# One factor chain for two layer norms in a fused attention and expert kernel, with ScalarE's normalizations at other steps

## The reference

```python
x = layernorm(x + attention(x))      # 16 heads of 8, causal
# feed-forward:
xn = (x - mu) / sqrt(var + 1e-5) * gamma + beta
combine, idx = top2_gate(xn, Wg)     # 8 experts, two for each token
out = sum_e gate_e * (gelu(xn @ W1[e] + b1[e]) @ W2[e] + b2[e])
x = layernorm(x + (x + out))
```

## Time and profile before

| what | value |
| --- | --- |
| median of 3 runs | 1116.17 us (1111.87 to 1117.45) |
| the profiled execution | 1118.13 us |
| its span, first to last instruction | 1116.4 us |
| PE busy | 966.8 us (87%) |
| DVE busy | 830.4 us (74%) |
| ACT busy | 665.9 us (60%) |
| POOL busy | 683.8 us (61%) |
| mean granted TensorE clock | 0.964 of full speed |

### The profile page before, as it was taken

The page is one execution under the profiler, slowest core; times in us unless marked ns, Lnnn a source line. Parts: engine busy times, 40 slices in busy tenths (PEclk is TensorE's granted clock), DMA queues, the critical chain, the costliest instruction groups (busy, mean ns, idle before and its releaser), DMA issues.

```text
span 1116.4 us, 29852 instructions
## 1 busy us (share of the span) xinstructions
PE 966.8 (87%) x9185; PEld 640.2 (57%) x9185; DVE 830.4 (74%) x2262; ACT 665.9 (60%) x1338; POOL 683.8 (61%) x1063
## 2 busy tenths in 40 slices
PE   3789999999999989999999999879899889998750
PEld 1344454454545545544455455349899879997740
DVE  4777878888888898898888888974455455467744
ACT  1256657666666676676666766646475745556552
POOL 7022445775766766756657667666668546557874
PEclk9699999999999999999999999979899999999985
DMA  7523133143242342432432423343222223265515
GB/s 168 186 74 115 57 96 121 50 138 102 65 137 91 87 128 64 121 122 51 138 101 66 134 74 98 117 139 89 71 73 71 78 67 87 71 200 183 166 54 169
DMA packets 134569, 117.75 MB, mean 105 GB/s; under 512 B 56218, under 2 KB 99777, under 8 KB 134240
## 3 DMA queue, kind: packets, MB, share of 16 engines
q1 hardware_dynamic: 121808, 96.37, 29.7%
q0 software_dynamic: 8704, 17.06, 4.5%
q10 hardware_dynamic: 3904, 2.43, 0.9%
HBM read 65.26 MB, written 53.81 MB: 107 GB/s over the span
## 4 chain that ended last, share of the span: by engine, by line
PE 43%; DVE 18%; POOL 11%; issue 10%; ACT 7%; DMA 6%; SPq 4%; ACTq 1%; DVEq 0%; POOLq 0%
PE ring L1132 9%; PE ring L1148 9%; DVE negmax L1192 8%; PE ps_v L1072 5%; PE ring L1009 4%; PE ring L1040 4%; ACT probs L730 3%; POOL probs L598 2%; PE ring L1055 2%; SPq L397 2%; POOL rows_d L610 2%; PE ps_m L937 2%; POOL y_d L640 2%; DMA rows<-att_d 2%; PE ps_m L902 2%
## 5 line engine op out<-in xcount | busy, mean ns | idle before, releaser
L730 ACT ACTIVATE probs<-ring 128x768 f32<-128x768 f32 (+1 forms) x384 | 337.3, 883 | 213.5 <-PE ring L1009 212.5
L1192 DVE TENSOR_REDUCE negmax<-ring 128x2 f32<-128x1024 f32 (+3 forms) x512 | 409.3, 812 | 67.5 <-PE ring L1055 63.8
L598 POOL TENSOR_SCALAR_AFFINE_SELECT probs<-probs 128x512 f32<-128x512 f32 x256 | 163.6, 639 | 247.5 <-ACT probs L730 245.4
L840 ACT ACTIVATE vpad<-ring,b_s 128x128 f32<-128x128 f32 x576 | 165.0, 371 | 107.8 <-PE ring L1132 105.9
L640 POOL DMA_INDIRECT y_d<-vpad,xs x144 | 146.1, 1015 | 102.3 <-DVE vpad L1496 75.4
L1009 PE MATMUL ring<-qarea,kside 64*128 64x512 f32 (+3 forms) x1024 | 178.6, 387 | 24.0 <-DVE negmax L1192 18.0
L1040 PE MATMUL ring<-kside,qarea 64*128 64x256 f32 (+2 forms) x1024 | 166.5, 363 | 28.8 <-ACT probs L730 15.1
L1009 PEld LDWEIGHTS ring<-qarea,kside 64*128 64x128 f32 x1024 | 87.3, 187 | 179.3 <-issue 118.8
L1072 PE MATMUL ps_v<-probs,vpad 128*32 128x512 f32 (+3 forms) x2048 | 180.4, 448 | 1.8 <-POOL probs L598 1.8
L1148 PE MATMUL ring<-qarea,vpad 128*128 x1152 | 157.5, 280 | 20.1 <-ACT vpad L840 20.0
L1132 PE MATMUL ring<-vpad,w_t 128*128 128x128 f32 x1152 | 157.1, 280 | 8.8 <-issue 8.6
(11 more groups left out here) (178 smaller groups left out, 1162.8 us busy)
## 6 DMA issues: line engine op xcount, KB each, us to landing
qk_d<-qarea SPq DMA_DIRECT2D x62, 256.0 KB, 2.6
kside<-qk_d SPq DMA_DIRECT2D x96, 128.0 KB, 3.0
qarea<-qk_d SPq DMA_DIRECT2D x90, 128.0 KB
xs<-rows_d SPq DMA_DIRECT2D x144, 66.0 KB, 1.9
probs<-y_d SPq DMA_DIRECT2D x16, 512.0 KB
xin<-L_attn_x SPq DMA_DIRECT2D x16, 256.0 KB, 3.0
att_d<-attt SPq DMA_DIRECT2D x128, 32.0 KB
rows<-att_d SPq DMA_DIRECT2D x16, 256.0 KB
```

What stands on the lines that cost most here:

```text
L598: pool.affine_select(out=diag, in_=diag, pattern=[[0, 4], [1, P]], compare_op=ALU.is_ge, fill=0.0, base=0, channel_multiplier=-1).then_inc ...
L730: nc.scalar.activation(of_unit(h // 2, part), ring[:, 2 * part % 3, :, (0, P, P)[part]:S], ACT.Exp, scale=SCALE).then_inc(sem("exp_done"), 1)
L840: ins = nc.scalar.activation(ht[:, n % 4, c, :], ps_a[:, n % 4, c * P:(c + 1) * P], ACT.Gelu_apprx_tanh, bias=b1_s[:, bass.ds(e, 1), c:c + ...
L1192: ins = nc.vector.tensor_reduce(negmax[:, n // 6 % 2, qb, s:s + 2], ring[:, (2 * n + 1) % 3, :, c0:c0 + nk], AX.X, ALU.max, negate=True)
```

## The change

Statistics are taken of ysum alone. GpSimd's chain at step 14 works out both norms' factors from them, on arrays twice as wide (two norms x 4 groups): the first factor from v + eps, the second, for y directly to xc, from v(1 + eps) + eps^2; the first is then doubled, so that x2 = 2 x1 comes straight from ysum. x1 is gone, as are the second statistics, the second chain and the doubling on GpSimd. ScalarE makes xc from ysum at steps 1 and 5 (at u = 0 and u = 2 of each) and x2 from ysum at steps 9 and 11. VectorE's write of ysum at step 12 and GpSimd's chain at step 14 wait for x2 of the block before. copy_v moves from the middle of step 4 to the head of step 5. SP stores x2 after the load of the attention output; in the last iterations at step 13 instead of 5.

```diff
--- before.py
+++ after.py
@@ -132,7 +132,6 @@
         attt = sb("attt", [P, S])
         rows16 = sb("rows16", [P, S])
         ysum = sb("ysum", [P, QB, D])
-        x1 = sb("x1", [P, QB, D])
         x2 = sb("x2", [P, QB, D])
         xc = sb("xc", [P, QB, D])
         xn = sb("xn", [P, 2, QB, TOPK, ROW])
@@ -149,9 +148,10 @@
         pasth = sb("pasth", [P, 3 * P // 2], BF16)
         lowerb = sb("lowerb", [P, P], BF16)
         onesb = sb("onesb", [P, P], BF16)
-        stats = sb("stats", [P, 2, QB, 6])
-        mv = sb("mv", [P, 2, QB, 2])
-        rs = sb("rs", [P, 2, 6, QB])
+        stats = sb("stats", [P, QB, 6])
+        mv = sb("mv", [P, QB, 2])
+
+        rs = sb("rs", [P, 6, 2, QB])
         halfneg = sb("halfneg", [P, QB])
         lg = sb("lg", [P, QB, E])
         rt = sb("rt", [P, 12, QB, E])
@@ -376,9 +376,9 @@
                     place_side(sp, nxt, 0, 0)
                     place_side(sp, nxt, 0, 1)
             if i.loop or i.value < NB:
-                store_x2(sp, prev.plus(-1))
                 store_attention(sp, prev)
                 load_attention(sp, prev)
+                store_x2(sp, prev.plus(-1))
 
         def store_x2(sp, b):
             if not b.exists(NB):
@@ -485,7 +485,7 @@
                         load_tile(m)
                 if not i.loop and i.value >= NB:
                     for h in range(NH):
-                        if h == 5:
+                        if h == 13:
                             store_x2(sp, i.plus(-2))
                         if h == 8:
                             store_attention(sp, i.plus(-1))
@@ -620,16 +620,9 @@
                                            ALU.add).then_inc(sem("xbo_ready"), 1)
                     if prev.exists(NB) and h == 14:
 
-                        need(pool, sem("x1_ready"), 1, prev, 0, sem("pool_passed"))
-                        rstd(pool, prev, 0)
-                    if rb.exists(NB):
-                        if h == 3:
-                            need(pool, sem("xc_ready"), 1, rb, 0, sem("pool_passed"))
-                            rstd(pool, rb, 1)
-                        if h == 4:
-
-                            need(pool, sem("x2_stored"), 16, rb, 0, sem("pool_passed"))
-                            pool.tensor_scalar(x2[:], x1[:], 2.0, None, ALU.mult).then_inc(sem("x2_ready"), 1)
+                        need(pool, sem("x2_ready"), 1, prev, 0, sem("pool_passed"))
+                        need(pool, sem("xc_ready"), 1, prev, 0, sem("pool_passed"))
+                        rstd(pool, prev)
                     for n in expert_steps(i, h):
                         send(n - 1)
 
@@ -642,22 +635,27 @@
                     ys[:, n % RING, :], None, bounds_check=T * TOPK - 1,
                     oob_is_err=False).then_inc(sem(f"sent{n % RING}"), 16)
 
-            def rstd(pool, b, which):
-
-                need(pool, sem(f"var{which}"), 1, b, 1, sem("pool_passed"))
-                v, r, s, t, n, m = (rs[:, which, k, :] for k in range(6))
-                pool.tensor_scalar(n, mv[:, which, :, 0], -1.0, None, ALU.mult)
+            def rstd(pool, b):
+
+
+                need(pool, sem("var"), 1, b, 1, sem("pool_passed"))
+                v, r, s, t, m = (rs[:, k] for k in range(5))
+                n, var = rs[:, 5, 0], mv[:, :, 1]
+                half = across(halfneg[:], 2)
+                pool.tensor_scalar(n, mv[:, :, 0], -1.0, None, ALU.mult)
+                pool.tensor_scalar(v[:, 0], var, EPS, None, ALU.add)
                 for k, step in enumerate((
-                        lambda: pool.tensor_scalar(v, mv[:, which, :, 1], EPS, None, ALU.add),
-                        lambda: pool.tensor_tensor(r, v, halfneg[:], ALU.pow),
+                        lambda: pool.tensor_scalar(v[:, 1], var, 1.0 + EPS, EPS * EPS, ALU.mult, ALU.add),
+                        lambda: pool.tensor_tensor(r, v, half, ALU.pow),
                         lambda: pool.tensor_tensor(s, r, r, ALU.mult),
                         lambda: pool.tensor_tensor(s, s, v, ALU.mult),
                         lambda: pool.tensor_scalar(s, s, -0.5, 1.5, ALU.mult, ALU.add),
                         lambda: pool.tensor_tensor(t, r, s, ALU.mult),
-                        lambda: pool.tensor_tensor(m, n, t, ALU.mult))):
+                        lambda: pool.tensor_scalar(t[:, 0], t[:, 0], 2.0, None, ALU.mult),
+                        lambda: pool.tensor_tensor(m, across(n, 2), t, ALU.mult))):
                     if k:
-                        need(pool, sem(f"rstd{which}"), 7, b, k, sem("pool_passed"))
-                    step().then_inc(sem(f"rstd{which}"), 1)
+                        need(pool, sem("rstd"), 8, b, k, sem("pool_passed"))
+                    step().then_inc(sem("rstd"), 1)
 
             def make_rows(pool, b, part):
 
@@ -731,16 +729,19 @@
                                                      ring[:, 2 * part % 3, :, (0, P, P)[part]:S],
                                                      ACT.Exp, scale=SCALE).then_inc(sem("exp_done"), 1)
 
-                        if u != 1 and h in (0, 1) and rb.exists(NB):
-                            if h == 0 and u == 0:
-
-                                need(act, sem("x2_ready"), 1, rb, 0)
-                            normalize(rb, 0, 2 * h + u // 2, x1, ysum, "x1_ready")
-                        if u != 1 and h in (5, 6) and rb.exists(NB):
-                            if h == 5 and u == 0:
-
+                        if h == 5 and u == 0 and nxt.exists(NB):
+                            copy_v(act, nxt)
+                        if u != 1 and h in (1, 5, 9, 11) and rb.exists(NB):
+                            if h == 1 and u == 0:
+
+                                need(act, sem("rstd"), 8, rb, 8)
                                 need(act, sem("xn_ready"), 1, rb, 0)
-                            normalize(rb, 1, 2 * (h - 5) + u // 2, xc, x1, "xc_ready")
+                            if h == 9 and u == 0:
+
+                                need(act, sem("x2_stored"), 16, rb, 0)
+                            second = h < 9
+                            normalize(rb, int(second), 2 * (h in (5, 11)) + u // 2, xc if second else x2,
+                                      "xc_ready" if second else "x2_ready")
                         if u == 1:
                             middle(act, h, i, nxt, prev, rb)
                             if h % 4 == 2:
@@ -767,11 +768,9 @@
                 nc.scalar.activation(to[:, :, 0, :, 0:HD], of[:, :, 0], ACT.Copy)
                 nc.scalar.activation(to[:, :, 1, :, 16:16 + HD], of[:, :, 1], ACT.Copy).then_inc(freed("v"), 1)
 
-            def normalize(b, which, q, dst, src, done):
-                if q == 0:
-                    need(act, sem(f"rstd{which}"), 7, b, 7)
-                ins = nc.scalar.activation(dst[:, q, :], src[:, q, :], ACT.Identity,
-                                           bias=rs[:, which, 5, q:q + 1], scale=rs[:, which, 3, q:q + 1])
+            def normalize(b, which, q, dst, done):
+                ins = nc.scalar.activation(dst[:, q, :], ysum[:, q, :], ACT.Identity,
+                                           bias=rs[:, 4, which, q:q + 1], scale=rs[:, 3, which, q:q + 1])
                 if q == QB - 1:
                     ins.then_inc(sem(done), 1)
 
@@ -787,8 +786,6 @@
                         need(act, ready("xT"), 1, nxt, 1)
                         need(act, ready("v"), 1, nxt, 0)
                         nc.scalar.activation(xt[:], ps_m[:], ACT.Copy).then_inc(freed("xT"), 1)
-                    if h == 4:
-                        copy_v(act, nxt)
                     if h == 3:
                         need(act, ready("qT"), 1, nxt, 1)
 
@@ -1238,16 +1235,16 @@
                     nc.vector.tensor_tensor(att[:, :, 64 * k:64 * k + 64].rearrange("p q (a d) -> p q a d", d=HD),
                                             of[:, :, :, 0:HD], along(urec[:], HD), ALU.mult).then_inc(freed("uT"), 1)
 
-            def statistics(b, which, src):
+            def statistics(b):
                 for q in range(QB):
-                    ins = nc.vector.bn_stats(stats[:, which, q, :], src[:, q, :])
+                    ins = nc.vector.bn_stats(stats[:, q, :], ysum[:, q, :])
                 ins.then_inc(sem("stats"), 1)
 
-            def aggregate(b, which):
-                need(dve, sem("stats"), 2, b, which + 1, sem("dve_passed"))
+            def aggregate(b):
+                need(dve, sem("stats"), 1, b, 1, sem("dve_passed"))
                 for q in range(QB):
-                    ins = nc.vector.bn_aggr(mv[:, which, q, :], stats[:, which, q, :])
-                ins.then_inc(sem(f"var{which}"), 1)
+                    ins = nc.vector.bn_aggr(mv[:, q, :], stats[:, q, :])
+                ins.then_inc(sem("var"), 1)
 
 
 
@@ -1381,19 +1378,14 @@
                             if at == 24:
                                 need(dve, ready("wo"), 1, prev, 1)
                                 need(dve, sem("xbo_ready"), 1, prev, 1)
```

(11 more changed lines are left out.)

## The result

The changed kernel takes **1108.81 us** (median of 9 runs, 1104.55 to 1115.06); the kernel before, run beside it, 1117.45 (9 runs, 1111.87 to 1119.98). The ratio is 0.9933, with a 95% interval of 0.9909 to 0.9957: faster by 0.67%. The profiled execution of the changed kernel took 1104.55 us (span 1102.5), that of the kernel before 1118.13 (1116.4).

A forecast was written before the change was run, and what follows sets the result against it. TensorE's own sequence was taken to bound the kernel, with 2.8 us of waiting per 43.8 us period; -6.7 - 3.8 + 0.7 + 1.7 = -8.1 us gave 1110.0 profiled, 1108.0 as median, range 1101 to 1115.5.

The forecast's parts named there:

- rival 1: Steps 0 and 1: GpSimd's later mask and xbo addition hold VectorE's routing products, losing step 0's gain; 1116.0 us, chance 0.24.
- Step 0 loses chain and normalizations, -6.7: ScalarE, step 0: xt and the second exponential come earlier, so TensorE's waits for exponentials nearly vanish in 14 periods; -6.7 us.
- Second statistics, -3.8: VectorE, steps 2 and 3: without these statistics TensorE's v product no longer waits for q's low part, 13 periods; -3.8 us.
- GpSimd's chain, growth 1.7, +0.7 us: GpSimd, step 14: chain grows by 1.7, delaying step 15's mask for step 1's value products in half the periods; +0.7 us.
- ScalarE's other places, 0: ScalarE, normalizations at other steps and copy_v behind step 4's exponential: gain up to 0.13 a period, loss up to 0.1; counted 0.
- SP's store, +1.7: Block 15's period: SP's store of x2 waits for step 11's normalizations and delays w2 loads and first experts' tiles; +1.7 us.
- The last mask of block 15, later by the growth, runs in parallel with it: End of attention part: block 15's last mask, delayed by GpSimd's longer chain, overlaps SP's store delay; no cost of its own.
- Rival 2: VectorE's small products beat GpSimd's masks elsewhere in the period: some 0.5 us in 12 periods, -6, giving 1102; chance 0.13.
- the predicted 42.9 to 43.2: Sign of the forecast: the steady period should last 42.9 to 43.2 us instead of 43.8.
- Rival 3: Step 14's chain grows beyond about 2.7, its mask holds step 1's value products; at 3.5 growth +12.5, 1128.7 us; chance 0.08.

The follow-up runs named there:

- the last four kernels: Changed kernel plus three edits (routing product, last mask, late store), 0.9875; plus late gate products, 0.9866; changed kernel with doubled power, 1.0067; three edits plus earlier ucp, 0.9841.

## Why the prediction was right, and where its steps were not

The forecast was 1108.0 us, the result 1108.81, inside the range, and on the side that had most of the chance. The sum is right because of two terms that were right and of misses that cancelled, and the closeness is in part luck: the copy of v and the statistics brought some 4 us more than forecast (3 and 1.2), and the held products of rival 1 took about 3.5 back, by the run with L1264 moved (0.9902 against 0.9933).

- *Step 0 loses chain and normalizations, -6.7.* Right in its mechanism: no row for exponentials is left where 6.4 us stood, and the experiment with two normalizations at step 0 brings the wait back. The size of this term alone was not measured.
- *Second statistics, -3.8.* Right in mechanism; some 5 us by the experiment, 4.7 by its periods.
- *GpSimd's chain, growth 1.7, +0.7 us.* The growth is 1.2: the power takes 1.68 instead of the 1.9 assumed, and the other operations don't grow with the width (0.20 at 4 and at 8). No value product waits for it in the steady periods. In the changed kernel's long period the mask ends at 430.82 and the products start at 431.56, 0.74 later.
- *ScalarE's other places, 0.* This step failed in its copy_v: the place is worth about 3 us. The bound was a gain of 0.13 a period; the trace shows 0.17, and the lost race on top. The step looked at each exponential's own wait and not at what follows from a later start.
- *SP's store, +1.7.* The size is near the +2.2 of the first product, and SP's own delay was 1.9; the failed step was "The last mask of block 15, later by the growth, runs in parallel with it". In the kernel before, the two chains that lead to the experts ended nearly together:

```profile
749.63 0.27 DVE L1488 COPY vpad<-ps_v 128x128 f32<-128x128 f32 x1
...
750.10 0.47 PE L1122 MATMUL ps_v<-ident,xs 128*128 128x128 f32 x1 [1.74 <-DMA xs<-rows_d]
```

The tile loads were last there, by 0.2 us over the copy behind mask, value products and ucp. After the change the mask's chain is last: the row of this place waits for vpad. TensorE's wait for the mask, 1.78, became 4.00, by the growth of 1.2 and by 1.0 that TensorE came earlier against the chain (before, its preceding products ended 1.95 behind the chain's start; now 0.92), and the halved clock cost the 32 products 2.1 more. The 1.0 is of this execution: four traces of changed kernels have the 1.95 and wait 3.0. Counted from the last xt, the chain started 0.9 earlier, grew by 1.2, and with the 2.1 the products ended 2.4 later (92.18 against 89.78); the first expert product followed at +2.2. The store's delay lay beneath: TensorE went on 3.0 to 3.9 us behind the first tile load's issue where it waited for it (three traces), so with an issue at +90.31 the loads alone would have held the first product until +93.5 to +94.4 by my estimate, 0.3 to 1.2 later than before. The wait of 1.78 was in the trace of before and could have been read there.
- *Rival 1*, VectorE takes back the gain of step 0, is partly true. Held products cost TensorE 0.87 in each long period; but the kernel keeps the rest. The mechanism given, mask and xbo addition on the routing products, is the one in the rows of 425.40 to 432.04.
- *Rival 2*, the lead wins a race, is the other half of the same: in the short periods VectorE comes first. Forecast and both rivals are mixed in one execution, period by period: the mean of 43.14 lies in the predicted 42.9 to 43.2, and neither of the two kinds does.
- *Rival 3*, the chain becomes the bound. The doubled power shows it. "The point is a growth of about 2.7: from there the mask of step 15 holds the value products" has the break-even right and the onset wrong. The wait begins at a growth of 2.86 - 0.97, about 1.9 by my estimate (in the long period at 425.4 a growth of 1.2 leaves 0.74, which gives the same), because TensorE itself is earlier against the chain; at 2.86 it has eaten the gain, and periods are as long as before. The tail's first product, 5.3 us later than before, comes on top; the measured 0.67% is 7.7 us, so some 2 us are left open.

## What to carry to other kernels

A wait taken away is worth what the next one in line leaves: the same edit of one routing product gave 0.1% before this change and 0.3% after it (in periods: nothing, and 0.65 us in each that lost the race), and taking away 10 us of waits for maxima gave nothing. When a chain on a queue grows, look through the iterations at the loop's ends and not only at the steady one: what is hidden in the middle may be the path there, or within 0.2 us of it. Where a period falls into two values, look for two instructions on engines that hold each other up, starting within a few hundredths of each other, and move one of them away.

## What the runs showed of the hardware

The granted clock fell behind waits at two places. In 14 traces the 32 value products of the last block took 2.36 to 2.38 us where TensorE had waited 0.18 to 1.78 us ahead of them (five traces), and 3.67 to 4.50 where it had waited 2.65 to 5.23 (nine traces). Against the trace of before, 1.28 us more of waiting (3.06) came with 2.13 more for the products. The length of the wait alone doesn't decide: with two normalizations at step 0, TensorE waited 1.43 at 317.6 and the clock fell to 0.50, and it waited 1.43 at 408.1 and the clock stayed at 1.00.

GpSimd's power costs 1.05 us for 128x4 and 1.68 for 128x8, that is, by my estimate from these two widths, 0.16 us for each element of a partition above some 0.4 fixed; a product or sum takes 0.20 at either width.

In the nine traces where L1264 (L1267 before the change) stands at its place, it started 0.03 to 0.04 us behind the mask in the 28 periods in which it took 0.17, and 0.03 to 0.07 behind in the 86 in which it took 0.61 to 0.63. The Trainium skill (SBUF — State Buffer, Who interferes with whom) says that the order of issue decides who is blocked, and that the other one is blocked wholly. For the second the rows agree: the product of 425.40 ends 0.05 behind the mask's end. For the first they can't be used: by the recorded starts the mask is first both at 382.87, where it takes 0.71, and at 425.36, where it takes 0.62. The one row that goes further is L1285, which was held for 1.97 us, as long as a mask (0.65) and a product (1.29) one behind the other.

The chips of the last four kernels took 1145 and 1148 us for the kernel before where the others took 1116 to 1117. In the kernels profiled there, the part up to the last xt was as long as elsewhere; from the first expert product to the end they took 392.9 to 396.5 us instead of 361.6 to 366.9. TensorE's idle time without a releaser in the profile ("issue") at the experts' first product was 21.3 to 36.4 us there and 8.5 in the changed kernel's trace. What is behind it stays open.
